# Adjacency loads issued by ACT, SP left with the transposes of E

## The chip, the cores and the metric

The kernel runs on one core of a Trainium2 chip. The metric is the device time of one execution in microseconds (us). Before the change it is 695.29, the median of three runs (692.45 to 695.46).

## The reference

x is 4096 x 128, adj is 4096 x 4096 of zeros and ones, all in 32-bit floats. Two layers, each with a residual and a layer norm:

```python
deg = clip(adj.sum(axis=1), 1.0);  dis = deg ** -0.5
diffusion = (dis[:, None] * adj * dis[None, :]) @ x - x
sim = x @ x.T / (norms[:, None] * norms[None, :])
attn = softmax(beta * sim * adj, axis=1)
x = layernorm(x + diffusion + sigmoid(alpha) * (attn @ x - x))
x = layernorm(x + relu(adj @ (x @ weights)))
```

## The kernel before

The 4096 nodes are 32 rows of 128 (R = 32). One instruction stream is written by hand for each engine, and semaphores tie the streams together. There are two phases.

The attention phase goes through the 32 rows. For a row r of 128 nodes the work is this:
- The adjacency of the row, 128 x 4096 floats, comes from DRAM in four pieces of 1024 columns, 512 KB each, into the buffer `land`, which holds one row: four pieces, one slot each (`land_piece`, line 238). ACT casts each piece to bytes (`cast`, line 418), with a weight per piece. A slot is free for the next row as soon as its cast is done, which `cast_done` counts.
- POOL adds the four byte pieces into packed words (`pack`, 306), TensorE turns them (`turn_adj`, line 931, matmuls of line 939, one pair a row), and DVE stores them (`store_adj`). The whole adjacency so stays in SBUF as `packT` for the second phase.
- TensorE makes the cosines in eight banks of 512 (`cosines`, 943, line 955), and DVE masks each bank by the bytes and takes its maximum (`mask`, 652, line 662). ACT takes the exponentials in four pieces in the order 2, 3, 0, 1 (`exps`, 461, line 466). Piece 2 waits for the row's maximum.
- E, the row of exponentials, has to be turned before `E @ x`. Its first half (pieces 0 and 1) is turned by TensorE in four blocks (`turn_e`, 959, line 966) and split into a high and a low 16-bit part by ACT (`e_high`, 469, line 473) and DVE (`e_low`, line 677). The second half (pieces 2 and 3) is split first, by POOL (`ex_high`, line 326) and DVE (`ex_low`, line 683), and then turned by two DMA transposes into `eTx` (`turn_ex`, 241, line 244), one per piece, n = 0 and n = 1. The parts of a piece, `e_parts`, are free for the next row when its transpose has landed.
- TensorE multiplies the turned E with x in eight steps (`attend`, 970, lines 987 and 990), the last of them during the next row.

The engines' streams are staggered. In the step h = 0..7 of ACT's `row(r)` (line 476), ACT does e_high of row r at every even h, the casts of row r + 2 at h = 0..3, and the exponentials of row r + 1 at h = 4..7. ACT's loop (line 495) holds two rows, POOL's two, TensorE's two, DVE's eight (line 791), SP's four (line 260). Rows outside the loops are written out.

SP issued all DMAs. Its order in the loop, for each row: pieces 0 and 1 of the adjacency, each as soon as its slot was cast; the transpose n = 1 of one row; pieces 2 and 3; the transpose n = 0 of the next row.

The start, to about 60 us: norms, the unit rows and their turn, the scaled parts of x in 16 bits (`x_high` on ACT, lines 434 and 458; `x_low` on POOL, line 346), while the first rows of adjacency are cast.

The second phase, from about 457 us, multiplies the turned adjacency with the scaled x and, after layer 1, with x @ weights (line 1044), 32 rows each. It has no adjacency loads and no DMA transposes; SP stores the results.

Of the kernel before, what the change touches and what calls it, by code (L numbers as in the profile page):

```python
# [37 lines left out]
K = 4  # L38
# [12 lines left out]
def two_layer_gnn(nc, x, adj, alpha, beta, weights, out):  # L51
    N, D = x.shape
    R = N // P
    B = R // K
    CH = 1024
    C = N // CH
# [11 lines left out]
    with ExitStack() as ctx:  # L68
# [161 lines left out]
        def _(sp):  # L230
# [6 lines left out]

            def land_piece(b, k, i):

                sp.dma_start(land[:, i, :], adj_v[b, k, :, i * CH:(i + 1) * CH]).then_inc(land_full[i], 16)  # L240
            def turn_ex(r, q, n):
# [5 lines left out]

            for i in range(C):
                land_piece(0, 0, i)
            for k in range(1, K):  # L250
                for i in range(C):
                    sp.wait_ge(cast_done, (k - 1) * C + i + 1)
                    land_piece(0, k, i)
                    if k == K - 1 and i == 1:
                        turn_ex(0, 0, 1)
                if k == K - 2:
                    turn_ex(0, 0, 0)
                if k == K - 1:
                    turn_ex(1, 1, 0)
            with sp.Fori(1, B) as b:  # L260
                for k in range(K):
                    r, q = b * K + (k - 3), (k + 1) % 2
                    for i in range(C):
                        sp.wait_ge(cast_done, b * (K * C) + ((k - 1) * C + i + 1))
                        land_piece(b, k, i)
                        if i == 1:
                            turn_ex(r, q, 1)
                    turn_ex(r + 1, 1 - q, 0)
            for r in (R - 3, R - 2, R - 1):
                turn_ex(r, r % 2, 1)  # L270
                if r < R - 1:
                    turn_ex(r + 1, (r + 1) % 2, 0)
            sp.wait_ge(e_turned, R * TB)
# [123 lines left out]
        def _(act):  # L397
# [15 lines left out]
            def norm_root(q):  # L413
                act.wait_ge(norms2_done, q + 1)
                nc.scalar.activation(norm[:, q * TC:(q + 1) * TC], norm[:, q * TC:(q + 1) * TC], ACT.Sqrt,
                                     scale=1.0 / (XN_SCALE * XN_SCALE)).then_inc(root_done, 1)

            def cast(r, q, i, first=False):

                if not first:  # L420
                    act.wait_ge(packed_done, r - 1)
                act.wait_ge(land_full[i], r * 16 + 16)
                nc.scalar.activation(adj_bytes[:, q, i * CH:(i + 1) * CH], land[:, i, :], ACT.Copy,  # L423
                                     scale=float(BYTE_ONE >> i), accum_out=deg[:, i, bass.ds(r, 1)]).then_inc(cast_done, 1)
# [25 lines left out]
            for g in range(4, H):  # L450
                turned_high(g)
            for i in range(1, C):
                cast(0, 0, i, first=True)
            act.wait_ge(small_loaded, 32)
            nc.scalar.activation(e_alpha, alpha_c, ACT.Exp, scale=-1.0).then_inc(alpha_exp, 1)
            cast(1, 1, 0, first=True)
            act.wait_ge(scales_done, 1)
            x_high(0)
            x_high(2)

# [14 lines left out]

            def row(r, q, start=False):

                for h in range(H):
                    if h % 2 == 0:
                        e_high(r, h // 2, start)  # L480
                    if h < C:
                        cast(r + 2, q, h)
                    else:
                        exps(r + 1, 1 - q, EXP_ORDER[h - C])

            exps(0, 0, 2)
            exps(0, 0, 3)
            cast(1, 1, 1, first=True)
            exps(0, 0, 0)
            exps(0, 0, 1)  # L490
            cast(1, 1, 2, first=True)
            cast(1, 1, 3, first=True)
            row(0, 0, start=True)
            row(1, 1)
            with act.Fori(2, R - 3, 2) as r:
                row(r, 0)
                row(r + 1, 1)

# [634 lines left out]
```

## Time and profile before

| | |
|---|---|
| profiled execution | 693.76 us |
| its span | 691.9 us |
| TensorE busy | 660.2 us (95%) |
| DVE busy | 562.5 us (81%) |
| ACT busy | 436.0 us (63%) |
| POOL busy | 237.4 us (34%) |
| share of the chain on TensorE | 83% |
| loads of adjacency | 128 of 512 KB, 4.6 us to landing (median) |
| transposes of E | 64, 4.5 us to landing (median) |

The shares are over the whole span. ACT, DVE, POOL and the DMAs do most of their work in the first 450 us. Issuing a DMA, register steps, branches and waits are done by an engine's queue and do not count as busy. Where a view tells of them it writes SPq, ACTq or DVEq. "Idle before, releaser" is the time an engine stood still just before an instruction, and what ended it; "issue" is a wait for nothing that the profile shows.

### The profile page before, as it was taken

The page shows a single profiled execution, that of the slowest core. Times are in us where ns is not written, and L with a number is a line of the kernel's source. Part 1 is how long each engine was busy: PE and PEld are TensorE (multiplying, and loading weights), DVE is VectorE, ACT ScalarE, POOL GpSimd, SP SyncE. Part 2 cuts the span into 40 slices and gives each one's busy share as a digit, 9 for nine tenths or more (in the row PEclk, how much of TensorE's full clock was granted, in tenths as well). Part 3 has the DMA queues.
Part 4 walks back from the last instruction along what each step waited for, and adds up shares of the span by engine and source line. Part 5 has one row for each costly group of instructions (what it writes and reads, how often), then busy time and mean ns, then how long its engine had stood idle before and what let it go on. Part 6 is the DMA issues. An engine that isn't in the chain of part 4 may idle for free.

```text
span 691.9 us, 18090 instructions
## 1 busy us (share of the span) xinstructions
PE 660.2 (95%) x5651; PEld 522.5 (76%) x5651; DVE 562.5 (81%) x1684; ACT 436.0 (63%) x879; POOL 237.4 (34%) x219
## 2 busy tenths in 40 slices
PE   7788999998999998999999999699999999999997
PEld 7455777776777776777777777598888888888886
DVE  6767999997899997999999899876777676666664
ACT  6986898898698998798898997712222223111111
POOL 3597346555345545346445455600000000000000
PEclk9989999999999999999999999999999999999999
DMA  7497999999799999899999995400000000000000
GB/s 271 160 243 184 223 270 248 254 265 234 195 259 250 244 265 246 220 244 252 257 254 241 256 247 106 77 5 1 0 0 0 0 0 1 16 15 30 15 15 31
DMA packets 154551, 105.41 MB, mean 152 GB/s; under 512 B 135696, under 2 KB 136208, under 8 KB 154512
## 3 DMA queue, kind: packets, MB, share of 16 engines
q1 hardware_dynamic: 154512, 105.01, 59.6%
q14 instruction: 29, 0.24, 0.1%
q8 instruction: 10, 0.16, 0.1%
HBM read 69.34 MB, written 2.10 MB: 103 GB/s over the span
## 4 chain that ended last, share of the span: by engine, by line
PE 83%; DVE 5%; POOL 4%; issue 3%; ACT 3%; DMA 2%; SPq 1%; DVEq 0%; POOLq 0%; ACTq 0%
PE ps_e L1044 30%; PE ps_s L955 20%; PE ps_e L987 7%; PE ps_e L966 7%; PE ps_acc L987 7%; PE ps_e L990 4%; PE ps_acc L990 3%; DVE e_parts L683 1%; DMA eTx<-e_parts 1%; POOL x_parts L349 1%; PE ps_e L1004 1%; PE ps_at L939 1%; PE ps_s L1004 1%; POOL u L372 1%; POOL e_parts L326 1%
## 5 line engine op out<-in xcount | busy, mean ns | idle before, releaser
L955 PE MATMUL ps_s<-xn_parts,xn_signed 128*128 128x512 f16 x756 | 207.5, 385 | 9.7 <-DVE cmax L662 6.8
L662 DVE CUSTOM_DVE_ANT_1 scores<-ps_s,adj_bytes 128x512 f32<-128x512 f32 x252 | 171.7, 682 | 33.2 <-issue 18.0
L466 ACT ACTIVATE scores<-scores,col 128x1024 f32<-128x1024 f32 x128 | 157.4, 1232 | 6.6 <-DVE col L673 6.2
L326 POOL TENSOR_SCALAR e_parts<-scores 128x1024 f16<-128x1024 f32 x64 | 78.1, 1220 | 177.8 <-ACT scores L466 115.2
L423 ACT ACTIVATE adj_bytes<-land 128x1024 uint8<-128x1024 f32 x128 | 133.5, 1047 | 0.7 <-DMA land<-in_adj 0.7
L1044 PE MATMUL ps_e<-x_parts,stage 128*128 128x256 f16 x1024 | 113.0, 273 | 0.0
L1044 PEld LDWEIGHTS ps_e<-x_parts,stage 128*128 128x128 fp8e4 x1024 | 100.2, 98 | 11.5
L473 ACT ACTIVATE eT_parts<-ps_e 128x512 f16<-128x512 f32 x128 | 75.7, 591 | 49.3 <-PE ps_e L966 48.7
L955 PEld LDWEIGHTS ps_s<-xn_parts,xn_signed 128*128 128x128 f16 x756 | 70.4, 99 | 47.0 <-DVE cmax L662 8.7
L1044 PE MATMUL ps_e<-y_parts,stage 128*128 128x256 f16 x896 | 105.4, 273 | 0.1
L1044 PEld LDWEIGHTS ps_e<-y_parts,stage 128*128 128x128 fp8e4 x896 | 87.2, 98 | 10.5 <-issue 0.9
L683 DVE SCALAR_TENSOR_TENSOR e_parts<-scores,e_parts 128x1024 f16<-128x1024 f32 x64 | 92.5, 1446 | 2.7 <-POOL e_parts L326 2.7
L733 DVE TENSOR_SCALAR stage<-packT 128x256 uint32 (+2 forms) x256 | 58.2, 287 | 41.4 <-PE ps_e L1044 41.4
L677 DVE SCALAR_TENSOR_TENSOR eT_parts<-ps_e,eT_parts 128x512 f16<-128x512 f32 x128 | 87.6, 684 | 3.1 <-ACT eT_parts L473 3.1
L966 PE MATMUL ps_e<-ident,scores 128*128 128x128 f32 x512 | 78.8, 277 | 5.1 <-ACT scores L466 5.0
L523 ACT ACTIVATE col<-mv,col 128x1 f32<-128x1 f32 x64 | 18.6, 290 | 97.7 <-DVE mv L824 97.7
L557 ACT ACTIVATE scores<-ps_e,col 128x128 f32<-128x128 f32 x32 | 11.8, 368 | 88.5 <-PE ps_e L1044 88.5
L966 PEld LDWEIGHTS ps_e<-ident,scores 128*128 128x128 f32 x512 | 54.9, 142 | 8.9 <-ACT scores L466 5.7
L987 PE MATMUL ps_acc<-x_parts,eTx 128*128 128x256 f16 x256 | 49.2, 273 | 2.2 <-DMA eTx<-e_parts 2.2
L987 PE MATMUL ps_e<-x_parts,eTx 128*128 128x256 f16 x256 | 49.9, 276 | 0.7 <-DMA eTx<-e_parts 0.7
L987 PE MATMUL ps_acc<-x_parts,eT_parts 128*128 128x256 f16 x256 | 49.8, 275 | 0.3 <-DVE eT_parts L677 0.3
L987 PE MATMUL ps_e<-x_parts,eT_parts 128*128 128x256 f16 x256 | 49.7, 275 | 0.0
(131 smaller groups left out, 997.9 us busy)
## 6 DMA issues: line engine op xcount, KB each, us to landing
land<-in_adj SPq DMA_DIRECT2D x128, 512.0 KB, 4.6
x_keep<-in_x SPq DMA_DIRECT2D x4, 512.0 KB, 5.1
out<-u SPq DMA_DIRECT2D x7, 256.0 KB, 2.0
eTx<-e_parts SPq DMA_TRANSPOSE x64, 4.5
out<-u SPq DMA_DIRECT2D x1, 192.0 KB, 1.9
eT_parts<-in_L_gnn_weights SPq DMA_DIRECT2D x1, 64.0 KB, 7.5
scores<-in_L_gnn_weights SPq DMA_DIRECT2D x1, 64.0 KB, 1.8
out<-u SPq DMA_DIRECT2D x1, 64.0 KB, 1.6
```

The lines of the kernel that those rows point to most:

```text
L326: nc.gpsimd.tensor_scalar(e_parts[:, n, 0, :], scores[:, q, (n + 2) * CH:(n + 3) * CH], E_SCALE, 1.0, ALU.mult, ALU.mult).wait_op(sign_don ...
L423: nc.scalar.activation(adj_bytes[:, q, i * CH:(i + 1) * CH], land[:, i, :], ACT.Copy, scale=float(BYTE_ONE >> i), accum_out=deg[:, i, bass ...
L466: nc.scalar.activation(piece, piece, ACT.Exp, bias=neg_max[q], scale=abs_beta, accum_out=csum[:, q, i:i + 1]).then_inc(exp_done, 1)
L473: nc.scalar.activation(eT_parts[:, b, 0, :], ps_e[:, b % 2, :], ACT.Copy, scale=E_SCALE).then_inc(e_hi, 1)
L662: nc.vector.tensor_tensor_reduce(scores[:, q, o:o + BANK].rearrange("p (k q) -> p k q", k=K), score_bank(h, r == 0 if start else False).re ...
L677: nc.vector.scalar_tensor_tensor(eT_parts[:, b, 1, :], ps_e[:, b % 2, :], E_SCALE, eT_parts[:, b, 0, :], ALU.mult, ALU.subtract).then_inc( ...
L683: nc.vector.scalar_tensor_tensor(e_parts[:, n, 1, :], scores[:, q, (n + 2) * CH:(n + 3) * CH], E_SCALE, e_parts[:, n, 0, :], ALU.mult, ALU ...
L733: nc.vector.tensor_scalar(stage[:, bass.ds(n, 1), i * CH // K:(i + 1) * CH // K], packT[:, bass.ds(r, 1), :], i, BYTE_ONE * 0x01010101, AL ...
L955: ins = nc.tensor.matmul(score_bank(h, start), xn_signed[:, q, part, :], xn_parts[:, other, o:o + BANK], start=(part == 0 and other == 0), ...
L966: ins = nc.tensor.transpose(ps_e[:, b % 2, n * P:(n + 1) * P], scores[:, q, t * P:(t + 1) * P], ident[:, :])
L987: nc.tensor.matmul(attn_ps[q][:, 0:2 * D], hi, x_parts[:, t, :], start=(k == 0 and n == 0), stop=(k == H - 1 and n == TH - 1), skip_group_ ...
L1044: return nc.tensor.matmul(ps_e[:, n, 0:2 * D], lhs[:, b, :, k], y[t], start=(t == 0), stop=(t == R - 1))
```

## The change

ACT issues the adjacency loads of all rows but the first. Each is placed in ACT's stream after an instruction that follows the cast of that slot: in `row`, piece h - 1 after step h, for h = 1..4. ACT waits for `cast_done` of the slot and then issues. SP keeps the four loads of row 0 and, in plain order, the 64 transposes. The attention loop of ACT now holds four rows, in six passes, with four rows written out behind it; SP's loop holds four transposes.

```diff
@@ SP
-            def land_piece(b, k, i):
-                sp.dma_start(land[:, i, :], adj_v[b, k, :, i * CH:(i + 1) * CH]).then_inc(land_full[i], 16)
+            for i in range(C):
+                sp.dma_start(land[:, i, :], adj_v[0, 0, :, i * CH:(i + 1) * CH]).then_inc(land_full[i], 16)
...
-            for i in range(C):
-                land_piece(0, 0, i)
-            for k in range(1, K):
-                for i in range(C):
-                    sp.wait_ge(cast_done, (k - 1) * C + i + 1)
-                    land_piece(0, k, i)
-                    if k == K - 1 and i == 1:
-                        turn_ex(0, 0, 1)
-                if k == K - 2:
-                    turn_ex(0, 0, 0)
-                if k == K - 1:
-                    turn_ex(1, 1, 0)
-            with sp.Fori(1, B) as b:
-                for k in range(K):
-                    r, q = b * K + (k - 3), (k + 1) % 2
-                    for i in range(C):
-                        sp.wait_ge(cast_done, b * (K * C) + ((k - 1) * C + i + 1))
-                        land_piece(b, k, i)
-                        if i == 1:
-                            turn_ex(r, q, 1)
-                    turn_ex(r + 1, 1 - q, 0)
-            for r in (R - 3, R - 2, R - 1):
-                turn_ex(r, r % 2, 1)
-                if r < R - 1:
-                    turn_ex(r + 1, (r + 1) % 2, 0)
+            turn_ex(0, 0, 0)
+            turn_ex(0, 0, 1)
+            turn_ex(1, 1, 0)
+            with sp.Fori(1, R - 2, 2) as r:
+                turn_ex(r, 1, 1)
+                turn_ex(r + 1, 0, 0)
+                turn_ex(r + 1, 0, 1)
+                turn_ex(r + 2, 1, 0)
+            turn_ex(R - 1, 1, 1)
@@ ACT
+            def land_piece(b, k, i):
+                act.wait_ge(cast_done, b * (K * C) + ((k - 1) * C + i + 1))
+                act.dma_start(land[:, i, :], adj_v[b, k, :, i * CH:(i + 1) * CH]).then_inc(land_full[i], 16)
...
             for g in range(4, H):
                 turned_high(g)
+                if g == 4:
+                    land_piece(0, 1, 0)
             for i in range(1, C):
                 cast(0, 0, i, first=True)
+                if i >= 2:
+                    land_piece(0, 1, i - 1)
             act.wait_ge(small_loaded, 32)
             nc.scalar.activation(e_alpha, alpha_c, ACT.Exp, scale=-1.0).then_inc(alpha_exp, 1)
+            land_piece(0, 1, C - 1)
             cast(1, 1, 0, first=True)
             act.wait_ge(scales_done, 1)
             x_high(0)
+            land_piece(0, 2, 0)
             x_high(2)
...
-            def row(r, q, start=False):
+            def row(r, q, start=False, ahead=None):
                 for h in range(H):
...
                     else:
                         exps(r + 1, 1 - q, EXP_ORDER[h - C])
+                    if ahead and 1 <= h <= C:
+                        land_piece(ahead[0], ahead[1], h - 1)
...
             exps(0, 0, 0)
+            land_piece(0, 2, 1)
             exps(0, 0, 1)
             cast(1, 1, 2, first=True)
             cast(1, 1, 3, first=True)
-            row(0, 0, start=True)
-            row(1, 1)
-            with act.Fori(2, R - 3, 2) as r:
-                row(r, 0)
-                row(r + 1, 1)
+            land_piece(0, 2, 2)
+            land_piece(0, 2, 3)
+            row(0, 0, start=True, ahead=(0, 3))
+            row(1, 1, ahead=(1, 0))
+            with act.Fori(1, B - 1) as b:
+                for k in range(K):
+                    row(b * K + (k - 2), k % 2, ahead=(b, k + 1) if k < K - 1 else (b + 1, 0))
+            for k in range(K):
+                row(R - 6 + k, k % 2, ahead=(B - 1, k + 1) if k < K - 1 else None)
```

## Rows read from the trace of the kernel before

**Rows 1.** Stretch: us, busy PE PEld DVE ACT POOL (instructions), clock, DMA share, GB/s.

```profile
200.00:250.00 50.00, 50.00 (x427) 36.73 (x425) 47.85 (x123) 45.48 (x81) 25.79 (x24) 1.00 1.02 253
```

**Rows 2.** Timeline of TensorE, line 939 only: start, us, engine, instruction, out<-in, count.

```profile
167.88 0.39 PE L939 MATMUL ps_at<-ident,packed 128*128 128x128 f32 x2
...
184.51 0.39 PE L939 MATMUL ps_at<-ident,packed 128*128 128x128 f32 x2
...
349.73 0.39 PE L939 MATMUL ps_at<-ident,packed 128*128 128x128 f32 x2
...
362.19 0.39 PE L939 MATMUL ps_at<-ident,packed 128*128 128x128 f32 x2
...
375.51 0.39 PE L939 MATMUL ps_at<-ident,packed 128*128 128x128 f32 x2
```

**Rows 3.** The waits over the whole span: us in total, times, longest.

```profile
PE ps_s L955 <- DVE cmax L662: 6.8, 6, 2.3
...
PEld ps_e L987 <- DMA eTx<-e_parts: 3.0, 7, 1.2
...
PE ps_e L987 <- DMA eTx<-e_parts: 0.7, 1, 0.7
```

**Rows 4.** Timeline of ACT in one row of the attention phase.

```profile
208.89 1.05 ACT L423 ACTIVATE adj_bytes<-land 128x1024 uint8<-128x1024 f32 x1
...
211.67 0.60 ACT L473 ACTIVATE eT_parts<-ps_e 128x512 f16<-128x512 f32 x1 [0.60 <-PE ps_e L966]
...
214.73 0.60 ACT L473 ACTIVATE eT_parts<-ps_e 128x512 f16<-128x512 f32 x1 [0.39 <-PE ps_e L966]
...
215.88 1.24 ACT L466 ACTIVATE scores<-scores,col 128x1024 f32<-128x1024 f32 x1 [0.56 <-DVE col L673]
...
220.05 1.23 ACT L466 ACTIVATE scores<-scores,col 128x1024 f32<-128x1024 f32 x1
```

**Rows 5.** The chain that ended last, in order of time, in the same row.

```profile
220.29 0.65 PE ps_e L966 x4
```

**Rows 6.** Timeline of SP's queue in the same row.

```profile
210.61 1.91 SPq L244 DMA_TRANSPOSE eTx<-e_parts  x1
213.14 1.00 SPq L240 DMA_DIRECT2D land<-in_adj  x2
214.36 4.54 SPq L244 DMA_TRANSPOSE eTx<-e_parts  x1
```

**Rows 7.** The chain again, in the row from 362.19.

```profile
362.52 2.88 SPq L244
...
367.15 7.64 DMA eTx<-e_parts
```

**Rows 8.** SP's load issues, ns min/median/max, and the loads' time to landing.

```profile
L240 SPq DMA_DIRECT2D land<-in_adj x128: 328/339/1547, 4.3 to 410.3; - x128
...
DMA to landing us min/median/max: 3.4/4.6/10.2
```

**Rows 9.** ACT's queue at one branch back of its loop, ns min/median/max, when.

```profile
L495 ACTq COMPARE_BRANCH  x1: 45/45/45, 88.8 to 88.8; - x1
L495 ACTq FUSED_REGOPS  x1: 50/50/50, 88.9 to 88.9; - x1
```

**Rows 10.** Timeline of ACT's arithmetic then: the row's last exponential.

```profile
90.45 1.23 ACT L466 ACTIVATE scores<-scores,col 128x1024 f32<-128x1024 f32 x1
```

**Rows 11.** Timeline of POOL at the start.

```profile
26.50 4.22 POOL L349 TENSOR_TENSOR x_parts<-u,x_parts 128x1024 f16<-128x1024 f32 x2 [5.38 <-ACT x_parts L435]
```

**Rows 12.** DVE's queue at a branch back of its loop.

```profile
L791 DVEq COMPARE_BRANCH  x1: 68/68/68, 166.1 to 166.1; - x1
L791 DVEq FUSED_REGOPS  x1: 93/93/93, 171.1 to 171.1; - x1
```

**Rows 13.** Timeline of DVE: its next instruction after that branch.

```profile
171.59 0.69 DVE L662 CUSTOM_DVE_ANT_1 scores<-ps_s,adj_bytes 128x512 f32<-128x512 f32 x1 [3.49 <-issue]
```

**Rows 14.** SP's transpose issues, ns min/median/max.

```profile
L244 SPq DMA_TRANSPOSE eTx<-e_parts x64: 1704/2962/4987, 35.9 to 443.5; - x64
```

## The prediction

> **What bounds the kernel now.** I read the stretches first, then the timeline, the waits and the queues' own work. In the steady part of the attention phase TensorE never idles: 50.00 of 50 us, beside DVE 47.85 and ACT 45.48 [rows 1]. The two matmuls that turn a row's packed adjacency come once a row and serve as its clock: 349.73 to 362.19, so 12.46 us a row [rows 2]. The row from 362.19 takes 13.32, the one from 167.88 takes 16.63, and a second row of that kind comes some 104 us later. In the 16.63 TensorE waits 2.3 us for a mask of DVE; in the 13.32 it waits 0.7 us for a landed transpose [rows 3]. From about 457 us on the kernel is two dense layers with no adjacency load and no transpose in them, and the change can't touch that part. So the question is what the change does to some 28 rows of 12.46 us, to the start before them, and to the few long rows.
>
> ACT has little room. In the row shown it idles 0.60, 0.39 and 0.56 us ahead of three instructions [rows 4]. At the end of the row nothing is left: the exponentials that TensorE turns next end as the last instruction starts, at 220.05, and TensorE turns them at 220.29, as a piece of the chain [rows 4, 5].
>
> **The change, part by part.**
>
> *SP loses the loads.* Before, SP issued both kinds of DMA in order: two loads (1.00 us), a transpose (4.54 us), and so on [rows 6]. In the row of 13.32 the chain runs through this: one transpose is issued from 362.52 for 2.88 us, to 365.40; then come two loads; the next transpose leaves only at 367.15 and lands 7.64 us later [rows 7]. Without the loads it leaves up to 1.75 us sooner, with 1 MB less ahead of it on its ring. What is late next in that row is TensorE itself. The gain is 13.32 - 12.46 = 0.86 us, once. In the other rows TensorE has no such wait, and POOL's idle time behind landings is on no path that ends last. I take -0.9. Bounds: 0, and -3.0, which is every wait of a weight load in that group, seven of them, whether a matmul covered it or not [rows 3].
>
> *The same bytes move.* 512 KB a load, four a row, and two transposes a row: 253 GB/s [rows 1]. Loads are asked for about one cast later than before and are needed a row later, against a median of 4.6 us to landing and 10.2 at the worst [rows 8]. That 12.46 us covers both, so this costs 0. With the cover gone, each us that a load is late would be a us of ACT.
>
> *ACT gains the issues.* An issue held SP for 0.339 us [rows 8]; two issues in a row took 1.00 with the steps between them [rows 6]. Four a row are 1.36 us of issue, some 2 us of queue time. Whether ACT's arithmetic waits for it depends on whether its queue runs ahead. It does: ACT's loop branch was taken at 88.8, while the last exponential of the row ran from 90.45 to 91.68, so the queue was 2.9 us ahead [rows 9, 10]. Each load is placed behind an instruction of 1.05 or 1.24 us that has just been queued, and waits for the cast before it, which is done by then. Queued behind it on ACT are the next e_high, cast or exponentials, and DVE and TensorE wait for those. 0.34, or 0.5 with its steps, fits under 1.05: I take 0. From the other side, were nothing hidden, pieces 0 to 2 (1.0 us) would use up the idle 0.60 and 0.39, and piece 3, which stands ahead of the exponentials of rows 5, would add 0.34 to each of some 27 rows: +9.2 us. Below nothing no reason leads, as ACT does no less than before.
>
> *The start.* POOL makes the low parts of x from 26.50, after waiting 5.38 for ACT's x_high [rows 11]. From there POOL sets the pace until about 58. Four loads are now issued by ACT ahead of that x_high and one behind it. Hidden they cost 0; at the other end 4 x 0.34 = 1.4 us. I take +0.4, since the pieces ahead of them are partly short.
>
> *Longer loops on ACT.* Counted in the program, ACT's attention loop was about 75 instructions for two rows; four rows with sixteen issues are about 210. DVE's loop of eight rows has about 550. On DVE the branch back was taken at 166.1 and the next instruction came at 171.1: 5.0 us, of which DVE idled 3.49 [rows 12, 13]. On ACT, with the short loop, the next one came 0.1 us after the branch [rows 9]. For ACT's five branches back the bounds are 0 and 5 x (5.0 - 2.9) = 10.5 us. Two of the five fall where DVE stalls anyway (after rows 9 and 17), so at most 3 x 2.1 = 6.3 should count. I take +1.5, which is nearer to the short loop's 0.1, since the long loop is still under half of DVE's. The Trainium skill (Runtime: NRT & Kernel Launch, Instruction fetch mechanics) says that such an engine holds two blocks of 256 instructions, and that a taken branch to a target outside them waits for a fetch. DVE's 5.0 us agrees. By that rule a body of 210 that lies across a block boundary would miss too, and this term would be near the 6.3.
>
> *Sum.* -0.9 + 0 + 0.4 + 1.5 = +1.0 us on the profiled execution: 693.76 (a span of 691.9 and 1.86 around it) becomes 694.8. The median of the runs, 695.29, lies 1.5 above that execution, so I predict 696.3.
>
> **Rivals.**
>
> *The two queues get in each other's way (slower).* The place: a load that ACT issues while SP issues a transpose. SP's transposes take 1.7 to 5.0 us to issue, median 2.96 [rows 14]; in the row shown they take 1.91 and 4.54 out of 12.46 [rows 6]. If the one that issues holds something that the other needs, a load that comes second waits for the whole transpose and ACT's queue stands still. Piece 0 comes at about 210.0, when the first cast has ended (208.89 + 1.05), next to the transpose of 210.61. Piece 2 comes at about 213.3, when the third cast has ended (the e_high of 211.67, then 1.05 more), where a transpose without loads ahead of it would start. It decides once the wait outlasts what ACT has queued, about 1 us. A wait of 3 us at piece 2 makes the e_high of 214.73 late by about 2, against idle 0.39 and 0.56: +1 us a row, 27 rows, 722 us. A wait of 1.9 costs some 0.25 a row: 702. For it: transposes hold SP for 6.5 of 12.46 us, and the places coincide. Against it: SP alone issued, so nothing in the trace shows it; and a transpose took 1.91 with no load just ahead and 4.54 with two, so the long ones may get shorter. The Trainium skill (Perfetto Trace Analysis, "DMA Instruction — HWDGE (DVE, Sync)") states it outright: the descriptor generator is shared by the issuing sequencers, locked for exclusive use, and freed once all descriptors are made. No run here shows it yet.
>
> *The reload at ACT's loop in full (slower).* 2.1 us for each of three branches, less the 0.9: +5.4, 701. For it stands DVE's 5.0 us; against it, that DVE's masks leave some room before they need ACT's first e_high.
>
> *Nothing but the gain (no change).* If issues and branches hide fully: 695.29 - 0.9 = 694.4, within my forecast's own range.
>
> *A real gain (faster).* 695.29 - 3.0 = 692.3 is all that the waits on landings hold, 0.4%. More would need what the profile doesn't show, for instance quicker code fetches on DVE (16.63 - 12.46 = 4.17 us in the row of rows 2): 690.5 at the best.
>
> **How the numbers follow.** About 0.5% (3.5 us) is what a measurement of this kernel can tell from no change. The forecast (hidden issues, small loop cost), 692.5 to 698.7: 0.46. The queues in conflict, by more than 3.5 us: 0.30. The reload in full: 0.14. A gain over 3.5 us: 0.10. So faster 0.10, same 0.46, slower 0.44. The range goes from 692.4 to 712, which holds the forecast, the reload, and the conflict up to a little over half of its worst price. The likeliest case's own range is 692.5 to 698.7.
>
> **What would show it.** Right: 12.46 us between the pairs of rows 2, ACT's issues about 0.34 us long with its arithmetic back to back over them, and the row of 13.32 gone. The conflict would show as ACT issues of more than 1 us, idle time of ACT behind them, and rows of 12.7 to 13.5. The reload would show as about 5 us between ACT's branch and its next instruction, five times. I am wrong outright if even short issues hold up ACT's arithmetic (rows longer by 0.34), or if loads come late to their casts.

## The result and the profile after

The changed kernel takes 837.16 us (median of four runs, 824.2 to 845.54) against 694.2 for the one before. The ratio is 1.193, with a 95% interval from 1.182 to 1.204; it compares the two faster of the four runs (824.2 and 831.97) with the runs before, and the profiled run, 842.35, is one of the two slower. The prediction was 696.3 with a range to 712. It was too low by 141 us, and none of the rivals had named the cause.

The span of the profiled execution is 840.5 us: 148.6 more than before's 691.9. All of it lies in the attention phase. Between the first and the last pair of TensorE's turns of the packed adjacency lie 31 rows; they take 553.2 us after and 404.3 before, which is 148.9 more. The second phase is as long as it was.

The timeline of TensorE in the changed kernel, line 941 only (line 939 of before), answers to [rows 2]:

```profile
294.06 0.39 PE L941 MATMUL ps_at<-ident,packed 128*128 128x128 f32 x2
...
313.37 0.63 PE L941 MATMUL ps_at<-ident,packed 128*128 128x128 f32 x2
...
328.04 0.39 PE L941 MATMUL ps_at<-ident,packed 128*128 128x128 f32 x2
```

Rows of 19.31 and 14.67 us stand where 12.46 stood. Over all 31 they go from 12.8 to 26.4, and their mean is 17.8. The stretches (the columns are those of [rows 1]) show who works less:

```profile
200.00:250.00 50.00, 39.79 (x302) 27.97 (x299) 34.41 (x91) 33.29 (x59) 15.39 (x17) 0.88 0.82 160
300.00:400.00 100.00, 79.07 (x582) 55.13 (x582) 66.04 (x172) 65.12 (x114) 27.10 (x31) 0.90 1.05 179
```

Everybody. TensorE is busy 39.79 of 50 us where it was busy 50.00, its granted clock is down from 1.00, the level of 2.4 GHz, to a mean of 0.88 over that level and the one of 1.2, and the DMA engines carry 160 GB/s instead of 253 at a share of 0.82. No engine is busy all the time any more. Then who holds whom? The waits over the span answer to [rows 3]:

```profile
POOL e_parts L310 <- DMA eTx<-e_parts: 224.8, 35, 12.6
ACT eT_parts L468 <- PE ps_e L968: 199.5, 77, 11.6
...
DVE scores L664 <- issue: 118.1, 32, 10.5
...
PEld ps_acc L989 <- DMA eTx<-e_parts: 77.4, 19, 9.6
PE ps_acc L989 <- DMA eTx<-e_parts: 68.1, 19, 9.1
...
PE ps_e L989 <- DMA eTx<-e_parts: 45.9, 12, 8.1
```

TensorE's matmuls waited for landed transposes for 0.7 us in the bank ps_e [rows 3] and 2.2 in ps_acc (one wait, at 42.15 us, in the start); now they wait 45.9 and 68.1. The chain that ended last says the same: DMA has 34% of the span (eTx<-e_parts), where TensorE had 83%. This is a stretch of it, without the pieces of TensorE (start, us, what):

```profile
296.21 1.15 DVE e_parts L685
...
297.43 14.64 DMA eTx<-e_parts
```

SP issues the transpose 0.07 us after DVE has finished the parts, so SP is free and on time, as the change meant it to be. But the transpose lands after 14.64 us. TensorE's timeline shows what that does:

```profile
306.11 0.81 PE L957 MATMUL ps_s<-xn_parts,xn_signed 128*128 128x512 f16 x3
312.11 0.39 PE L989 MATMUL ps_acc<-x_parts,eTx 128*128 128x256 f16 x1 [5.19 <-DMA eTx<-e_parts]
```

The two kinds of DMA, each the row of its own issuing line (ns min/median/max, when) and its time to landing; they answer to [rows 8, 14]. First the transposes:

```profile
L244 SPq DMA_TRANSPOSE eTx<-e_parts x64: 1692/3548/10665, 35.8 to 592.0; - x64
...
DMA to landing us min/median/max: 4.3/9.2/19.1
```

And ACT's loads:

```profile
L405 ACTq DMA_DIRECT2D land<-in_adj x124: 334/344/756, 15.4 to 547.4; - x124
...
DMA to landing us min/median/max: 3.6/6.2/16.2
```

Transposes land after 9.2 us in the median, against 4.5 before. The two pieces differ, and one median hides it. Over rows 2 to 30 of the two traces, a transpose n = 0 landed after 4.3 us before and 8.7 after, a transpose n = 1, which before stood on the ring right behind two loads, after 6.7 and 11.3 (medians). The two transposes of [rows 6], asked for one by one:

```profile
L244 SPq DMA_TRANSPOSE eTx<-e_parts x1: 1907/1907/1907, 210.6 to 210.6; - x1
...
DMA to landing us min/median/max: 4.3/4.3/4.3
```

```profile
L244 SPq DMA_TRANSPOSE eTx<-e_parts x1: 4544/4544/4544, 214.4 to 214.4; - x1
...
DMA to landing us min/median/max: 6.6/6.6/6.6
```

Loads took longer too, 6.2 against 4.6, but ACT waited for one only once, for 0.6 us. And ACT's issues took 0.344 us each, under running arithmetic.

### The profile page after: what moved, and what is told of

Its sections match the earlier page's. It is cut to its first block, busy times and chain, and to the rows that moved or that the text cites. A ratio compares the mean times of both kernels' runs of the same rounds, so it can differ in the third digit from the quotient of the medians.

```text
span 840.5 us, 18007 instructions
## 1 busy us (share of the span) xinstructions
PE 703.8 (84%) x5651; PEld 543.4 (65%) x5651; DVE 558.4 (66%) x1684; ACT 437.7 (52%) x879; POOL 206.0 (25%) x219
## 2 busy tenths in 40 slices
DMA packets 154553, 105.42 MB, mean 125 GB/s; under 512 B 135696, under 2 KB 136208, under 8 KB 154512
## 4 chain that ended last, share of the span: by engine, by line
PE 48%; DMA 34%; DVE 8%; issue 7%; ACT 2%; POOL 1%; DVEq 0%; SPq 0%; ACTq 0%; POOLq 0%
DMA eTx<-e_parts 34%; PE ps_e L1046 25%; PE ps_s L957 7%; DVE e_parts L685 4%; PE ps_e L989 3%; PE ps_acc L989 3%; PE ps_e L968 2%; PE ps_e L992 2%; PE ps_acc L992 1%; DVE scores L664 1%; DVE eT_parts L679 1%; DMA x_keep<-in_x 1%; PE ps_e L1006 1%; PE ps_at L941 1%; PE ps_s L1006 1%
## 5 line engine op out<-in xcount | busy, mean ns | idle before, releaser
L957 PE MATMUL ps_s<-xn_parts,xn_signed 128*128 128x512 f16 x756 | 220.9, 405 | 4.1 <-DVE cmax L664 4.1
L310 POOL TENSOR_SCALAR e_parts<-scores 128x1024 f16<-128x1024 f32 x64 | 68.6, 1071 | 356.2 <-DMA eTx<-e_parts 224.8
L989 PE MATMUL ps_acc<-x_parts,eTx 128*128 128x256 f16 x256 | 54.3, 292 | 68.1 <-DMA eTx<-e_parts 68.1
L957 PEld LDWEIGHTS ps_s<-xn_parts,xn_signed 128*128 128x128 f16 x756 | 74.2, 104 | 45.6 <-issue 8.9
L989 PE MATMUL ps_e<-x_parts,eTx 128*128 128x256 f16 x256 | 53.4, 289 | 45.9 <-DMA eTx<-e_parts 45.9
L968 PE MATMUL ps_e<-ident,scores 128*128 128x128 f32 x512 | 83.4, 289 | 5.0 <-ACT scores L461 5.0
L685 DVE SCALAR_TENSOR_TENSOR e_parts<-scores,e_parts 128x1024 f16<-128x1024 f32 x64 | 84.6, 1321 | 1.8 <-POOL e_parts L310 1.8
L989 PEld LDWEIGHTS ps_acc<-x_parts,eTx 128*128 128x128 f16 x256 | 26.4, 103 | 86.1 <-DMA eTx<-e_parts 77.4
L989 PEld LDWEIGHTS ps_e<-x_parts,eTx 128*128 128x128 f16 x256 | 26.3, 103 | 61.3 <-DMA eTx<-e_parts 52.3
L968 PEld LDWEIGHTS ps_e<-ident,scores 128*128 128x128 f32 x512 | 59.0, 151 | 8.3 <-ACT scores L461 5.7
```

Of the source, the lines that this page charges most:

```text
L310: nc.gpsimd.tensor_scalar(e_parts[:, n, 0, :], scores[:, q, (n + 2) * CH:(n + 3) * CH], E_SCALE, 1.0, ALU.mult, ALU.mult).wait_op(sign_don ...
L685: nc.vector.scalar_tensor_tensor(e_parts[:, n, 1, :], scores[:, q, (n + 2) * CH:(n + 3) * CH], E_SCALE, e_parts[:, n, 0, :], ALU.mult, ALU ...
L957: ins = nc.tensor.matmul(score_bank(h, start), xn_signed[:, q, part, :], xn_parts[:, other, o:o + BANK], start=(part == 0 and other == 0), ...
L968: ins = nc.tensor.transpose(ps_e[:, b % 2, n * P:(n + 1) * P], scores[:, q, t * P:(t + 1) * P], ident[:, :])
L989: nc.tensor.matmul(attn_ps[q][:, 0:2 * D], hi, x_parts[:, t, :], start=(k == 0 and n == 0), stop=(k == H - 1 and n == TH - 1), skip_group_ ...
```

## The experiments

Theory A, formed on this trace: before, one ring (SP's) held both kinds of DMA in order, so a load that was asked for after a transpose didn't touch it. On two rings the later load runs at once, the 16 DMA engines take turns between the rings by packets, and a transpose, which is some 2,100 packets of 256 bytes (the 135,696 packets under 512 bytes on the profile's page, by 64 transposes), waits behind a load's packets of 4 KB. Its landing doubles. Rivals: the issues on ACT hold it up; ACT's longer loop; the DMA engines lack throughput with two rings.

**Transposes alone, on SP** (e1), as the loads stop after the first rows.

```diff
-                    row(b * K + (k - 2), k % 2, ahead=(b, k + 1) if k < K - 1 else (b + 1, 0))
+                    row(b * K + (k - 2), k % 2)
```

> The kernel after, without the adjacency loads of rows 5 to 31 (their casts read what row 4 left, so the output differs). Theory A (transposes are slowed by loads that run beside them on another ring): transposes land in 4.3 us as in the kernel before or sooner, rows take 12.46 us, and the time is 690 to 697. Theory B (the new order of SP's and ACT's streams is what costs): landings and rows stay as long as after, 800 us or more.

Measured: 701.4 us, 1.012 [1.006, 1.017]; transposes land in 4.3 us in the median; the rows are 12.45 or 12.46 us but for the two where DVE's loop comes round, and but for the first two, where the loads still run: they take 46.1 us together, as in the changed kernel (45.7; before 33.7). The time is over the 690 to 697 expected, and the start accounts for that. So the loss goes with the loads, and 12 us of it lie in the start. How the loads do it is left open by this.

**Plain copies in place of the transposes** (e2). The same bytes on the same two rings, ACT issues all loads; the second half of E isn't turned.

```diff
-                sp.dma_start_transpose(eTx[:, q, n, :, :],
+                sp.dma_start(eTx[:, q, n, :, :].rearrange("p a j -> p (a j)"),
```

> The kernel after with each DMA transpose replaced by a plain copy of the same 512 KB into the same place (E is then not turned, so the output differs). All issues, waits and both queues stay. Theory A (only transposes suffer beside loads): rows of 12.46 us and 690 to 698 us. Theory C (any two rings do): over 750 us. The rival of the prediction that ACT's issues hold up its arithmetic would show here as 700 us or more.

Measured: 691.38 us, 0.998 [0.995, 1.001]. Copies land in 4.7 us, loads in 5.2, and most rows are 12.45 or 12.46. That acquits ACT's 124 issues, its loop, and two rings as such. The damage needs a transpose beside the loads. A copy's packets are of 4 KB, a transpose's of 256 bytes, so whether it is the turning or the small packets that suffer is not separated by this.

**ACT's loop alone** (e3). The kernel before with the four-row loop on ACT, SP issuing everything.

```diff
-            with act.Fori(2, R - 3, 2) as r:
-                row(r, 0)
-                row(r + 1, 1)
+            with act.Fori(1, B - 1) as b:
+                for k in range(K):
+                    row(b * K + (k - 2), k % 2)
+            for k in range(K):
+                row(R - 6 + k, k % 2)
```

> The kernel before with only ACT's loop changed, four rows in a pass and four written out, all DMAs still issued by SP. My term for the longer loop was +1.5 us, the reload in full +6.3. The profile after shows 0.2 us between branch and next instruction, so I now expect no difference: 0.998 to 1.002 of before.

Measured: 693.76 us, 1.0005 [0.998, 1.003]. The loop costs nothing.

**The DMAs by themselves** (e0). A kernel with nothing but DMAs: ten rounds of each mix, each round begins when all of the last has landed. A round has the traffic of a row, four loads and two transposes. It computes nothing.

```python
rounds([L(0), L(1), T(4), L(2), L(3), T(5)], [])          # all on SP
rounds([T(4), T(5)], [L(0), L(1), L(2), L(3)])            # loads on ACT
rounds([L(0), L(1), L(2), L(3)], [T(4), T(5)])            # transposes on ACT
rounds([K(4), K(5)], [L(0), L(1), L(2), L(3)])            # copies on SP, loads on ACT
```

> All computation is left out; the kernel only moves data, in twelve phases of ten rounds. A round is four loads of 512 KB and two DMA transposes of 512 KB (or what the phase names), and starts when the last round has landed. Phases: transposes alone; loads alone from SP; loads alone from ACT; both from SP in the order of the kernel before; loads from ACT beside transposes from SP; loads from SP beside transposes from ACT; loads from ACT beside plain copies of the transposes' bytes from SP; loads and plain copies from SP; loads split between SP and ACT; both from ACT in the old order; 256 KB loads (2 KB rows) from ACT beside transposes from SP; the same from SP alone. Theory A (the two rings' packets mix in the DMA engines, and loads mixed with transposes slow both): the phases with both kinds on two rings take over 1.3 times those on one ring, whichever engine issues what; plain copies, split loads and everything from ACT alone stay within 10% of one ring. Theory B (something on ACT's side, its place in the stream or its waits): the phases differ by under 10%, since no computation is there. Theory C (any two busy rings slow each other): the plain copies and the split loads on two rings are slow too.

Measured, over all ten rounds of each (the first and third line from 235.6 to 378.3 and from 378.4 to 525.9 us), a round from its start to the next one's:

| mix | us a round | loads land | transposes or copies land |
|---|---|---|---|
| all on SP | 14.3 | 5.2 | 7.1 |
| all on ACT | 14.2 | 5.1 | 7.1 |
| loads ACT, transposes SP | 14.9 | 8.7 | 13.2 |
| loads SP, transposes ACT | 14.5 | 9.0 | 12.7 |
| loads and copies on SP | 11.6 | 6.9 | 7.8 |
| loads ACT, copies SP | 10.9 | 8.1 | 6.9 |

The rows of the two with loads and transposes, DMA issues (KB each, median us to landing). One ring:

```profile
land<-in_adj SPq DMA_DIRECT2D x40, 512.0 KB, 5.2
eTx<-e_parts SPq DMA_TRANSPOSE x20, 7.1
```

Two rings:

```profile
land<-in_adj ACTq DMA_DIRECT2D x40, 512.0 KB, 8.7
eTx<-e_parts SPq DMA_TRANSPOSE x20, 13.2
```

The expected loss of throughput isn't there: a round is 4% longer, not 30%. (With loads of 256 KB in rows of 2 KB it is 11%: 16.2 us against 14.6, transposes 11.7 against 6.3.) The latency of a transpose is what changes, 7.1 to 13.2 us, whichever engine issues it. It is that, much more than the bytes a second, that the second ring takes.

**One piece of four on ACT** (e5).

```diff
+    ON_ACT = (3,)
...
+                        if i not in ON_ACT:
+                            sp.wait_ge(cast_done, b * (K * C) + ((k - 1) * C + i + 1))
+                            land_piece(b, k, i)
```

> A mix of before and after: ACT issues only the fourth piece of each row (behind its exponentials of step 4, as after), SP issues the other three in the old order. Theory A (a load on the other ring overtakes a transpose that is under way, and each one that does costs it time): one load in four can overtake, so transposes land in 5 to 7 us in the median instead of 4.5 (before) and 9.2 (after), rows are 12.5 to 14.5, time 700 to 750. Theory D (with two rings busy the DMA engines collapse whatever the number of loads): close to after, over 780.

Measured: 770.4 us, 1.113 [1.109, 1.117], more than was expected of a quarter of the loads. The median landing is 4.9 us but the worst 14.4; rows swing between 12.5 and 20 us. One overtaking load a row is enough for long rows.

**ACT issues when the transpose has landed** (e6). Two rings, but ACT waits for the row's second transpose and then issues all four loads.

```diff
-                    if ahead and 1 <= h <= C:
-                        land_piece(ahead[0], ahead[1], h - 1)
+                if ahead:
+                    act.wait_ge(ex_turned[1], r * 16 + 16)
+                    for i in range(C):
+                        land_piece(ahead[0], ahead[1], i)
```

> The kernel after, with ACT issuing all four loads of a row together at the end of its step 7, once the row's second transpose (n = 1) has landed. Two rings as after, and the same number of issues on ACT, but hardly a load in flight beside that transpose. Theory A: transposes land in 4.3 to 5.5 us, rows are 12.5 to 13.5 (the first cast of the next row may come up to 1 us before its load has landed), time 694 to 725. Theory D: rows stay near the 17.6 us of after.

Measured: 721.01 us, 1.041 [1.038, 1.044]. Transposes land in 4.4 us (8.1 at the worst). Most rows are 13.1 to 14.5 us. ACT now waits for a load 84 times, 41.4 us in all, about 0.5 us at a time. That is not what the rows wait for: the chain goes through the transposes n = 0 of the next row, which still run beside the loads. They land in 6.2 us, and in 26 of the 29 rows from 2 to 30 TensorE waits for one. 116 of the 143 us (by the medians) come back by timing alone, with the same rings, engines and bytes.

**Loads in smaller packets** (e7 in 1 KB, e9 in 512 bytes, on two rings; e8 in 1 KB on one).

```diff
-        land = sb("land", [P, C, CH], F32)
+        land = sb("land", [P, C, 4, CH // 4 + 8], F32)
```

> The kernel after with each load landing in four runs of 256 floats per partition (with 32 bytes between them), so that a load's packets are 1 KB instead of 4 KB. Bytes, issues and rings stay. Theory A1 (the engines take turns by packet, and a transpose's 256-byte packet waits for one load packet each time; short load packets make that wait shorter): transposes land sooner than after's 9.2 us, and the time falls below 800. Theory A2 (what costs is each change between a load's packet and a transpose's packet): four times as many changes, so landings get longer and the time rises above 845.

> The kernel after with each load landing in eight runs of 128 floats, packets of 512 bytes. The 1 KB version took 725 us with transposes landing in 6.9. Theory A1: shorter still, 5.5 to 6.5 us and 700 to 722. If the loads themselves become too slow at 512 bytes, they show it by casts that wait for them, and the time is over 722.

> The kernel before, all DMAs on SP, with the loads in packets of 1 KB. On one ring the packets are served in order whatever their size. Theory A1: no change within 0.5% (ratio 0.995 to 1.005). If short packets help by something other than turns between rings, this kernel is faster than before by over 0.5%.

Measured: e7 725.01 us, 1.047 [1.038, 1.056], transposes 6.9 us; e9 726.6, 1.048 [1.042, 1.055], transposes 6.6 and loads 6.0; e8 696.67, 1.004 [1.002, 1.006], transposes 5.3. If the engines shared by bytes, or if the transposes themselves had become slow, the size of the loads' packets would not matter. It takes three quarters of the loss away, as turns by packets would; theory A2 is out. It stops there: 512 bytes bring nothing more, against what was expected, and the casts are not the reason, as ACT waited for a load once, for 1.8 us.

**The size by itself** (e11): the rounds of e0 with loads in packets of 4 KB down to 256 bytes.

```python
for m in (1, 2, 4, 8, 16):
    rounds([(f, 0), (f, 1), T(4), (f, 2), (f, 3), T(5)], [])
    rounds([T(4), T(5)], [(f, 0), (f, 1), (f, 2), (f, 3)])
```

> Computation left out, as in the first of these kernels: rounds of four loads of 512 KB and two DMA transposes, ten rounds a phase. The loads land in runs of 1024, 512, 256, 128 and 64 floats (packets of 4 KB down to 256 bytes); for each size one phase with all on SP in the old order and one with the loads on ACT. Theory A1 (the engines take turns by packet): with two rings the transposes land in about 13 us at 4 KB as before and sooner with each halving, towards the one ring's 7 us by 512 bytes, while the loads' own landings grow; with one ring the packet size changes the transposes' landings by under 20% down to 1 KB. Theory A2 (each change between kinds of packet costs): with two rings the transposes' landings grow as packets shrink.

| loads' packets | transposes, one ring | two rings | loads, one ring | two rings |
|---|---|---|---|---|
| 4 KB | 7.0 | 11.3 | 5.1 | 8.1 |
| 2 KB | 7.0 | 10.4 | 5.2 | 7.0 |
| 1 KB | 7.1 | 9.2 | 5.2 | 8.2 |
| 512 B | 6.6 | 9.4 | 5.0 | 8.4 |
| 256 B | 6.5 | 8.9 | 5.5 | 8.2 |

Medians in us over the ten rounds of each size. The price of the second ring shrinks from 4.3 us to 2.1 as the packets get as small as they were in e7, and then stays, where theory A1 expected it to be gone by 512 bytes. A floor would be there if a transpose, with equal packets too, still shares its engines with whatever the other ring holds; no run tests that. It fits that e9 gained nothing on e7. The mix of the first line is that of e0, where the price was 6.1 us (13.2 against 7.1); each was run once, and the 1.8 us between them is nearly the 2.2 by which the price falls here, so the table shows the direction better than the sizes.

**From a landing of 9 us to a row of 17.8.** I had taken this for the single buffer `e_parts`: POOL waited 224.8 us for it. e12 gives each row parity a buffer of its own (in space that the second phase uses later), with a semaphore for each; e13 is the same on before's one ring.

```diff
-                if not first:
-                    pool.wait_ge(ex_turned[n], r * 16)
+                if not (isinstance(r, int) and r < 2):
+                    pool.wait_ge(ex_turned[2 * q + n], r * 8 - 8 * q)
```

> The changed kernel with a second buffer for the parts of a piece (rows of even number use one, rows of odd number the other), so that POOL waits for the transpose of the row before last. Both queues stay as they are. Theory A (a transpose on its own ring is overtaken by loads, its landing doubles, and the single buffer makes that landing part of every row): transposes still land in 7 to 11 us in the median, POOL's wait for landings falls from 224.8 us to under 80, and the time from 837 to 705 to 770; what is left is TensorE's own wait for a landed transpose, which no buffer takes away. Theory D (the engines can't move the bytes in time when two rings are busy, whatever waits for what): rows stay at 16 to 18 us and the time above 800.

> The kernel before, with the same second buffer and all DMAs on SP. Under theory A the landing of about 4.5 us is hidden already, so 690 to 697: the rows stay at 12.46 us, and at best the two or three rows that wait for a transpose get shorter. If the single buffer held the kernel before back too, under 688.

Measured: e12 830.1 us, 1.194 [1.190, 1.198]; e13 693.78, 0.9995 [0.998, 1.002]. POOL's wait for landings is gone and the mean row is 17.7 us, against 17.8. The expectation under theory A was wrong, and theory D (throughput) was back in play, which foresaw this time. The chain of e12 points to the other way round the loop. First two transposes n = 1, each issued by SP as soon as DVE has split the piece, then TensorE's timeline:

```profile
278.75 1.15 DVE e_parts L689
279.97 11.03 DMA eTx<-e_parts
...
297.07 1.15 DVE y_parts L689
298.29 10.76 DMA eTx<-y_parts
```

```profile
293.30 0.28 PE L993 MATMUL ps_e<-x_parts,eTx 128*128 128x256 f16 x1 [3.65 <-DMA eTx<-e_parts]
...
310.54 0.34 PE L993 MATMUL ps_acc<-x_parts,eTx 128*128 128x256 f16 x1 [2.95 <-DMA eTx<-y_parts]
```

And the landing of the first of the two transposes:

```profile
L245 SPq DMA_TRANSPOSE eTx<-e_parts x1: 5489/5489/5489, 280.0 to 280.0; - x1
...
DMA to landing us min/median/max: 13.3/13.3/13.3
```

The chain's pieces of 11.03 and 10.76 us end before the landings: it leaves them for a stretch of DVE that it calls "issue", 4.76 us at 291.61. The landings themselves are where TensorE goes on. The transpose of 279.97 lands after 13.3 us, at 293.25, and 5.04 us later the next is issued, at 298.29; that one lands after 12.2, at 310.49, and after 5.20 us comes the issue of 315.69. Between landing and issue lies TensorE's work: it takes its instructions in order, so while it waits at `attend` for the landed transpose, the turns and cosines queued behind it wait too, and with them DVE's masks, the exponentials and the next split. e14 and e15 test whether delay alone makes such rows: transposes without loads (e1), each behind one or two DMAs of 512 bytes that SP waits for. Nothing competes for the DMA engines. As in e1, loads are left out.

```diff
                 sp.wait_ge(ex_lo, 2 * r + (n + 1))
+                for j in range(1):
+                    sp.dma_start(spare, beta.rearrange("(a o) -> a o", o=1).to_broadcast([P, 1])).then_inc(small, 16)
+                    sp.wait_ge(small, (2 * r + n) * 16 + 16 * (j + 1))
```

> The kernel of e1 (no loads beside the transposes in rows 5 to 31, 701.4 us), with one DMA of 512 bytes ahead of each transpose on SP, which SP waits for. It delays every landing by some 2 us and loads the DMA engines with nothing. Theory L (a late landing alone stretches the row, through TensorE's wait and what is queued behind it; a row is the landing plus about 7 us): the landing counts as some 6.5 us, the rows become 13 to 14 us and the time 715 to 740. Theory D (the DMA engines lack throughput when two rings are busy, and latency is hidden): the rows stay at 12.46 us and the time under 705.

> The same with two such DMAs, one after the other, so some 4 us of delay. Theory L: the landing counts as some 8.5 us, rows of 15 to 16 us, 765 to 810. Theory D: under 705.

Measured: e14 758.93 us, 1.095 [1.089, 1.101]; e15 869.19, 1.253 [1.248, 1.259], both longer than even theory L gave. Of the 65 and 175 us, 22 and 13 lie in the first two rows (55.9 and 46.6 us, against 33.7), which the expectation hadn't counted. The chain of e14, without TensorE's pieces:

```profile
303.90 2.48 DMA y_parts<-in_L_gnn_beta
...
306.44 4.28 DMA eTx<-e_parts
...
316.69 1.15 DVE e_parts L692
...
317.85 2.47 DMA y_parts<-in_L_gnn_beta
...
320.38 4.62 DMA eTx<-e_parts
```

The stretch from 300 to 400 us of e14:

```profile
300.00:400.00 100.00, 88.36 (x742) 63.60 (x740) 83.83 (x214) 80.55 (x141) 45.30 (x42) 1.00 0.40 73
```

And of e15:

```profile
300.00:400.00 100.00, 79.29 (x595) 54.94 (x595) 65.05 (x166) 63.95 (x112) 35.41 (x34) 0.91 0.32 58
```

These are transposes n = 0. The first has landed at 310.72 (306.44 + 4.28), and the next small DMA is issued at 317.85: 7.1 us of other work at full clock. A row is that plus 2.54 of delay plus 4.3, which is 13.9; the rows measured are 14.0 to 14.6. In e15 the DMA engines move 58 GB/s at a share of 0.32, and the rows are mostly 17.5 to 19.3 us, as long as the changed kernel's. The loop with e14's 7.1 would give 16.5 there, with 5.1 of delay, and 15 to 16 had been expected. In the chain of e15 the other work is longer: from the landing at 314.84 to the issue at 323.62 lie 8.8 us, in which TensorE's granted clock is 0.81, a mean over its two levels. What the clock and what SP's own busy queue add was not taken apart. So latency suffices for such rows (shown with delays that bind at n = 0; the changed kernel waits more often for n = 1), and theory D isn't needed. Against it also stands e7, which moves 227 GB/s over the same two rings from 300 to 400 us, where the changed kernel moves 179 at a share of 1.05. As a part of the loss it isn't excluded.

**DVE's loop written out** (e4 on the kernel before; e10 on two rings, with 512-byte packets).

```diff
-            with dve.Fori(0, G - 1) as n:
+            for n in range(G - 1):
```

> The kernel before, all DMAs on SP, with DVE's eight-row loop written out in full, so that DVE never branches back in the attention phase. In the prediction I put 16.63 - 12.46 = 4.17 us of one row down to the reload after that branch, with a second such row later (15.18). If so both go and 692.5 becomes 685 to 688: ratio 0.988 to 0.992. If the long rows have another cause, 0.998 to 1.002.

> The 512-byte version of the kernel after, with DVE's loop written out. If what is left over before in the two-ring version is the landings alone, this takes about 7 us off it: 693 to 715, and doesn't beat the written-out loop on one ring (685.3).

Measured: e4 685.3 us, 0.990 [0.988, 0.993]; e10 725.0, 1.047 [1.042, 1.051]. e4 is the best version here and beats both kernels. Its rows are 12.45 and 12.46 us where [rows 2] had 16.63. In e10, expected at 693 to 715, the gain doesn't show (725.0 against e9's 726.6); landings set the rows there.

## Why the prediction was wrong

**The step that failed** is *The same bytes move*, and with it the second half of *SP loses the loads*. The first put the loads' new place at 0, by bytes (253 GB/s as before) and by the loads' own slack. Both stood: ACT waited for a load only once, for 0.6 us. What it never asked is what the loads do to the *other* DMA. The second said that a transpose would leave sooner "with 1 MB less ahead of it on its ring", and counted that as a gain. The measured term is +4.7 us on the median landing (4.5 to 9.2), where I had it under nothing. The order on one ring was read as a cost to the transpose. A cost it was: without loads (e1) the transposes n = 1 land in 4.3 us instead of 6.7. But more than that it was a protection: on one ring a load could only delay a transpose that came after it.

**How 4.7 us got into the row.** From one transpose n = 1 to the next, a row is the landing, the time until TensorE uses what has landed, and the other work until the next issue. Before, these are 6.7, 0.5 and 5.4 us (medians of rows 2 to 30). The 0.5 is the slack, and it is why TensorE hardly waited for a landing [rows 3]. In the changed kernel they are 11.3, 0.05 and 5.3: in 18 of those 29 rows TensorE stands waiting when the transpose lands. In the means, which add up, the landing goes from 6.4 to 11.2 and the whole from 12.8 to 17.5, so the row grew by what the landing grew. For n = 0 the other work is longer, 7.1 us from use to issue, and the landing went from 4.3 to 8.7; TensorE waits for it in 11 of the 29. In e6 this second loop sets the rows (6.2 + 7.1 = 13.3 us; median 13.5). Beyond the first two rows (+12.0) 29 rows lost 136.9 us, 4.7 each. I had the number 4.5 in hand and the waits for landings, but neither the landings of each piece nor the loop they belong to; [rows 7], where one landing of 7.64 us made a row of 13.32, was that loop seen once, and I read it as something to gain. The lower clock goes with TensorE's waits: 0.88 in the changed kernel, 0.91 in e15 with hardly any DMA. Where it is low, the pair of matmuls at line 941 takes 0.63 us instead of 0.39.

**The rival on the slow side** (the queues in each other's way at the issue) had the right place and the wrong mechanism. I put the price on ACT, standing still behind SP's transposes. ACT's 124 issues took 0.334 to 0.756 us, though 90 of them began while SP was issuing a transpose, and those held SP for up to 10.7. No issue waited for a transpose's. The Trainium skill (Perfetto Trace Analysis, "DMA Instruction — HWDGE (DVE, Sync)"), which I weighed there, says that the generator is locked for exclusive use; in this trace no such wait is to be seen. The conflict is behind the issue, between the rings. The Trainium skill (DMA: Bandwidth & Descriptors, "Queues, rings and completion order") says that each DMA engine goes round its queues by whole packets. A packet there is a bundle of some 9 to 17 descriptors, and no run shows how that relates to the profile's packets of 256 bytes and 4 KB. In direction e7 agrees, as smaller packets of the loads took the landing from 9.2 to 6.9. I should have weighed this rule.

**ACT's issues, hidden: 0.** Right. In the timeline of ACT the issue lies over a running cast:

```profile
307.93 1.04 ACT L412 ACTIVATE adj_bytes<-land 128x1024 uint8<-128x1024 f32 x1
308.19 0.38 ACTq L405 DMA_DIRECT2D land<-in_adj  x1
```

**ACT's loop: +1.5.** It was 0 (e3), and ACT's queue goes on about 0.2 us after each branch. The rival of a full reload falls with it. The prediction also misread the rule of the Trainium skill (Runtime: NRT & Kernel Launch, Instruction fetch mechanics) that it cites: a body of 210 instructions touches at most two blocks of 256, and two are held, so by that rule it need not miss.

**The start: +0.4.** It was +12: the first two rows go from 33.7 us to 45.7. With ACT's loads held until the transpose has landed (e6) they take 33.7 again, so it is the same collision.

**The gain: -0.9, and DVE's stalls as the best case.** The -0.9 never had its condition, an earlier landing. e13 shows that POOL's wait for the buffer held nothing before (0.9995). The 4.17 us of one branch, which I put beyond what the profile shows, is there: e4 got 7.2 us (692.47 to 685.3) for two of them. "In the other rows TensorE has no such wait" overlooked the 2.2 us at 42.15 in the start, the sign that a late landing counts there too.

**Open.** Some landings reach 14 to 24 us (19.1 in the changed kernel, 23.8 in e12). That is more than a transpose's 4.3 us without loads and the 7.8 that the four loads of a row take by themselves in e0, and the engines' share stays near 1 while they move less; no run takes this apart. A plain copy in packets of 256 bytes beside the loads, which would tell small packets from the turning, was not run. Nor is it shown how much of a row's excess is latency and how much throughput: e12 can't tell one from the other, e14 and e15 only show that latency is enough.

## What to carry to other kernels

Two kinds of DMA on one ring are in an order, and this order can be what keeps a latency-bound transfer short; before moving one of them to another engine's queue, ask what it may now overtake and which loop the other's landing belongs to. Add up that loop, landing and all other steps to the next issue, and compare it with the row: the difference, about 0.5 us here, is all the delay that is free. Do it for each transfer of the row by itself, as a median over all of them hides the one that is late. A second buffer does not help where an engine that takes its work in order waits for the same landing.

## What the runs showed of the hardware

- A transpose of 512 KB beside 512 KB loads: lands in 7.1 us with all on one ring, in 13.2 on a ring of its own, in rounds of the same length within 4% (e0). Plain copies in its place don't suffer: 7.8 us on one ring and 6.9 on two, rounds of 11.6 and 10.9.
- Cutting the loads' packets from 4 KB to 1 KB cuts the second ring's price from 4.3 to 2.1 us, and smaller ones bring nothing more (2.8 at 512 bytes, 2.4 at 256) (e11).
- A DMA of 512 bytes takes 2.5 to 2.8 us to land, and its issue 0.337 (e14).
- How long DVE's queue stands at its loop's branch depends on what the DMA engines do: 5.0 us at both branches before [rows 12], 7.9 and 5.4 in the changed kernel, 2.9 and 3.1 without loads (e1), and 3.5 and 2.8 with plain copies on two rings (e2). In e1 the rows with the branches take 13.18 and 13.36 us, against 16.63 and 15.18 before.
